# The causal mask of the diagonal blocks: added by VectorE in PSUM, not by a product on TensorE

## The reference, cut to what matters

```python
# x: (4, 2048, 256) float32
Q = sign(x * sign(bv_q)); K = sign(x * sign(bv_k)); V = x * sign(bv_v)
scores = einsum('btd,bsd->bts', Q, K) * 256 ** -0.5
scores = where(causal, scores, -inf)
attn = where(causal, sigmoid(scores * 4.0), 0.0)
x = layernorm(x + einsum('bts,bsd->btd', attn, V))
# then: top-1 routing over 32 experts with a capacity, silu(g) * u, down, residual, layernorm
```

## Time and profile before

| | |
|---|---|
| median of the runs | 556.41 us (556.22 to 556.51, 3 runs) |
| span of the profiled execution | 556.1 us |
| TensorE busy | 523.5 us (94%) |
| VectorE busy | 407.6 us (73%) |
| ScalarE busy | 378.5 us (68%) |
| GpSimd busy | 373.8 us (67%) |
| the mask's products, L897 | 64, mean 219 ns |

### The profile page before, as it was taken

One profiled execution on the slowest core, in us unless ns is written; L12 is line 12 of the kernel. 1 busy time (PEld: TensorE's weight loads), 2 busy tenths in 40 slices (PEclk: granted clock), 3 DMA queues, 4 the chain that ended last, 5 costly groups with the idle time before them and its releaser, 6 DMA issues.

```text
span 556.1 us, 12156 instructions
## 1 busy us (share of the span) xinstructions
PE 523.5 (94%) x3990; PEld 458.8 (82%) x4028; DVE 407.6 (73%) x1026; ACT 378.5 (68%) x775; POOL 373.8 (67%) x497
## 2 busy tenths in 40 slices
PE   6999999999999999999999889999999999999970
PEld 5889888898988888988988448888888888888860
DVE  3774878866678857779575637888788888888870
ACT  5886968869778778688686306667667767677640
POOL 4647868777867778786773541677776777676772
PEclk9999999999999999999999999999999999999995
DMA  8994332254332632247911043666777776683200
GB/s 256 374 327 174 82 96 59 82 166 98 115 74 78 165 96 86 62 104 205 317 52 60 18 134 63 187 200 191 214 207 212 204 218 208 210 251 90 61 33 35
DMA packets 91902, 81.52 MB, mean 147 GB/s; under 512 B 31626, under 2 KB 83066, under 8 KB 91840
## 3 DMA queue, kind: packets, MB, share of 16 engines
q1 hardware_dynamic: 84848, 66.39, 41.3%
q0 software_dynamic: 6912, 14.30, 7.6%
q10 hardware_dynamic: 80, 0.07, 0.0%
HBM read 44.33 MB, written 37.90 MB: 148 GB/s over the span
## 4 chain that ended last, share of the span: by engine, by line
PE 84%; DVE 5%; issue 4%; POOL 3%; DMA 1%; ACT 1%; another core or an unknown queue 1%; DVEq 0%; POOLq 0%; SPq 0%; ACTq 0%
PE ps L918 11%; PE ps L919 10%; PE ps L920 10%; PE ps L894 9%; PE ps L1074 8%; PE ps L1082 7%; PE ps L1075 7%; PE ps L1100 5%; PE ps L1108 3%; PE ps L1047 2%; PE ps L937 2%; PE ps L1097 2%; PE ps L1099 1%; PE ps L1098 1%; DVE hl_ring L1170 1%
## 5 line engine op out<-in xcount | busy, mean ns | idle before, releaser
L918 PE MATMUL ps<-v_hl,hl_ring 128*128 128x256 f32 x544 | 175.8, 323 | 0.3 <-DVE hl_ring L1170 0.3
L919 PE MATMUL ps<-v_hl,hl_ring 128*128 128x256 f32 x544 | 153.4, 282 | 0.0
L920 PE MATMUL ps<-v_hl,hl_ring 128*128 128x256 f32 x544 | 153.1, 281 | 0.0
L918 PEld LDWEIGHTS ps<-v_hl,hl_ring 128*128 128x128 f32 x544 | 103.3, 190 | 15.8 <-issue 2.1
L1170 DVE TENSOR_TENSOR hl_ring<-ps,hl_ring 128x512 fp32r<-128x512 f32 (+3 forms) x160 | 93.3, 601 | 20.0 <-ACT ps L695 16.0
L919 PEld LDWEIGHTS ps<-v_hl,hl_ring 128*128 128x128 f32 x544 | 103.6, 190 | 2.4
L920 PEld LDWEIGHTS ps<-v_hl,hl_ring 128*128 128x128 f32 x544 | 103.2, 190 | 0.0
L693 ACT ACTIVATE hl_ring<-ps 128x512 fp32r<-128x512 f32 (+3 forms) x160 | 85.9, 537 | 20.5 <-PE ps L894 9.4
L695 ACT ACTIVATE ps<-ps 128x512 f32<-128x512 f32 (+3 forms) x160 | 87.1, 544 | 0.0
L619 POOL DMA_INDIRECT out_dram<-alone,ids x55 | 69.3, 1260 | 24.5 <-issue 18.8
L535 POOL DMA_INDIRECT expert_rows<-xrow,slot x64 | 64.3, 1005 | 29.2 <-issue 24.9
(11 more groups left out here) (163 smaller groups left out, 1095.8 us busy)
## 6 DMA issues: line engine op xcount, KB each, us to landing
expert_rows<-xs SPq DMA_DIRECT2D x40, 258.0 KB, 5.2
xs<-expert_rows SPq DMA_DIRECT2D x32, 258.0 KB, 3.1
xall<-in_L_attn_x_dram SPq DMA_DIRECT2D x16, 512.0 KB, 4.9
out_dram<-alone SPq DMA_DIRECT2D x16, 512.0 KB
xall<-in_L_ffn_w_gate_dram SPq DMA_DIRECT2D x32, 256.0 KB, 4.5
xall<-in_L_ffn_w_up_dram SPq DMA_DIRECT2D x32, 256.0 KB, 4.7
xall<-in_L_ffn_w_down_dram SPq DMA_DIRECT2D x32, 256.0 KB, 5.1
xs<-expert_rows SPq DMA_DIRECT2D x31, 64.5 KB
```

The source lines that it names most:

```text
L918: mm(o, ah, v_hl[:, 0, j, :], start=(j == 0 and i % 2 == 0), stop=False, skip_group_check=True)
L919: mm(o, ah, v_hl[:, 1, j, :], start=False, stop=False, skip_group_check=True)
L920: last = mm(o, al, v_hl[:, 0, j, :], start=False, stop=(j == GT * g + i), skip_group_check=True)
```

## The change

TensorE's third product of a diagonal step is gone. VectorE gets a new function, `mask(n)`: on a diagonal step it waits for the scores of step n and adds the mask to the 128 columns of the diagonal block, in place in PSUM; it signals `masked`. ScalarE's sigmoids of a diagonal step wait for `masked` and no longer for `scores_ready`. VectorE issues `mask` three steps ahead: right behind `low` of step n it stands for step n + 3, over the end of a batch too, ahead of whatever the tables put at step n; those of the first three steps stand in the prologue.

```diff
+AHEAD_MASK = 3
...
+        def masks_to(n):
+            return NT // B * (n // NS) + sum(j >= GT * g for g, j in STEPS[:n % NS])
...
 def weights(b, k):
-                act.wait_ge(scores_ready, n + 1)
+                if j >= GT * g:
+                    act.wait_ge(masked, masks_to(n) + 1)
+                else:
+                    act.wait_ge(scores_ready, n + 1)
...
 def scores(b, k):
-                diag = j >= GT * g
                 for c in range(DC):
                     last = mm(o, k_t[:, c, j * P:(j + 1) * P], q_t[:, g, c, lo:GQ],
-                              start=(c == 0), stop=(c == DC - 1 and not diag))
-                if diag:
-                    last = mm(ps[:, k % SB, lo:lo + P], identb[:, :], maskb[:, :], start=False, stop=True)
+                              start=(c == 0), stop=(c == DC - 1))
                 last.then_inc(scores_ready, 1)
...
+            def mask(n):
+                g, j, lo = cols(n % NS)
+                if j >= GT * g:
+                    dve.wait_ge(scores_ready, n + 1)
+                    o = ps[:, n % NS % SB, lo:lo + P]
+                    v_.tensor_tensor(o, o, maskb[:, :], ALU.add).then_inc(masked, 1)
...
 def batch(b, first, last):
                 for k in range(NS):
                     low(b, k)
+                    if b * NS + k + AHEAD_MASK < B * NS:
+                        mask(b * NS + k + AHEAD_MASK)
...
             v_.tensor_scalar(k_t[:, 1, 0:GQ], q_t[:, 0, 1, :], qk_sgn[:, 1:2], None, ALU.mult).then_inc(key_first, 1)
+            for n in range(AHEAD_MASK):
+                mask(n)
             dve.wait_ge(vh_first, 1)
```

More of the change, by code:

```diff
@@ L195, in bass_postln_attn_moe_kernel @@
         scores_ready = sem("scores_ready")
+        masked = sem("masked")
         a_ready = sem("a_ready")
```

## The result

| | before | changed |
|---|---|---|
| median of the runs | 556.46 us (556.22 to 556.55, 4 runs) | 564.86 us (563.75 to 569.01, 4 runs) |
| ratio, 95% interval | | 1.0164 (1.0132 to 1.0195) |
| span of the profiled execution | 556.1 us | 563.2 us |

The changed kernel is 8.4 us slower. The prediction was 568.7, with 560.3 to 576.5 as its range. The direction was right and the range holds the result, but the forecast loss was 12.3 us. The two places that should have made it up did not share it as predicted: one cost more, the other nothing. A later set of runs gave 575.8 for the same kernel, and there the second place cost what was predicted. Most of what follows is about that.

A forecast was written before the change was run, and what follows sets the result against it. TensorE was taken to bound the kernel. Terms -1.1 - 0.4 + 0.5 + 7.5 + 5.1 + 0.7 = +12.3 us on the 556.1 span gave 568.4, with 0.3 for the median 568.7 us; range 560.3 to 576.5.

The forecast's parts named there:

- The two places: Three batch ends, +7.5 us, and steps 17 to 20 of three batches, +5.1 us: predicted losses from VectorE waiting for scores.
- What bounds the kernel: Attention, four batches: TensorE bounds it, so removing 64 mask products there can win at most 6.2 us.
- (a): Three batch ends: next batch's first mask delays the gate, GpSimd, ScalarE and VectorE's subtraction; 2.5 us each, +7.5.
- The clock falls: Rival, chance 0.12: after the batch-end wait TensorE's clock halves, 2.5 us more at each of three boundaries; 576.2 us.
- (b): Steps 17 to 20: step 20's mask meets a late TensorE signal ahead of the router's pick; +1.7 in three batches, +5.1.
- signals in time: Rival, chance 0.22: the delay at steps 17 to 20 does not meet the new wait; 562.7 us.
- The first batch: Steps 17 to 20 of batch 1: no late signal there, so it keeps its saving of 0.39 us.
- (c): Steps 33 to 36: step 37's mask and the pick make S(39), step 39's scores, 0.25 late; +0.7 for four batches.
- (d): Steps 5 to 8: nothing comes late, 0.28 us kept in each of four batches, -1.1.
- (e): Kernel start: first sigmoid waits for a mask, three masks precede VectorE's first-values work; between 0.2 and 0.8, taken +0.5.

The follow-up runs named there:

- the most that can be won: The kernel before with its 64 mask products left out and nothing in their place, so diagonal blocks are unmasked: 553.88 us, ratio 0.9944.
- the filler kernel: The changed kernel plus 11 unused products of 512 columns on TensorE ahead of S(4), the scores of step 4, at three batch ends: 571.35 us.
- the last set: The changed kernel, nothing altered, run again on another chip beside the kernel before at 556.50 us: 564.64 and 564.94 us, ratio 1.0149.

## Why the prediction was right or wrong

*What bounds the kernel.* Right: where masks cost nothing, the time goes below before. The 6.2 us of "the most that can be won" was a count of groups, not of the path; 3.3 were measured. The sum did leave the saving out at the three batch ends, and it has none for the first group of batch 1 either, without a reason; without masks that group gives 0.01.

*(a) The batch end.* The chain over four engines and its durations held to 0.1 us in T(0), and moving two masks took 7.9 us back. Three boundaries at 2.7 and not 2.5 is 0.6 off. The step that was mis-sized is the 0.24 us of spare time that I took off in front of S(4). V(0) behind it waits for the residual sums (0.83 us from their start to its first product before, 0.82 after), and these have no spare time: they came the whole 2.5 later with T(0), and 0.21 more for the mask between. The term was 7.5 and measured 10.7; the other 2.6 are the clock.

*The clock falls.* I gave it 0.12 as a case of its own at 7.5 us. It fell at two of three boundaries for 3.4 us and cost 1.3 each time, as the filler kernel shows. The mechanism was right, the size was three times too large, and it is no case beside the others: it comes on top of (a). The Trainium skill, "TensorE: Matmul & The Clock Gate", section "HAM oscillation — how this bites in real kernels", describes a kernel that waits some 3 to 5 us between groups of products, and whose clock falls at every such wait. Here shorter waits, 2.65 us, did it at two of three places.

*(b) Steps 17 to 20.* In the first and the last set this step failed: -0.3 in place of +5.1, and the rival "signals in time", at 562.7, was the true case. I had read a delay of the trace of before as fixed to the step. It is real, the runs point to the scatter's traffic as its source, and the size was right (1.72, 1.77 and 1.79 for 1.73) where it occurs; but whether it occurs is not the kernel's alone. The argument "it stands at the same step in three batches" showed that it was systematic in one execution, no more.

*The first batch.* Predicted to keep 0.39, it lost 1.1. I asked what stands behind the mask at step 17 and not at step 20. There stands the copy of the fourth query group, which TensorE needs for S(24):

```profile
49.08 0.68 DVE L1157 COPY q_t<-ps 128x1024 bf16<-128x1024 bf16 x1
...
49.82 0.11 PEld L902 LDWEIGHTS ps<-q_t,k_t 128*128 128x128 bf16 x2 [1.52 <-DVE q_t L1157]
```

This is after, first set; in before the copy started at 46.33. With all masks behind the other work the stretch is -0.39; with only that of step 20 moved, +0.5.

*(c) Steps 33 to 36.* Predicted a loss of 0.2 a batch, it kept 0.4 where signals were in time; where they were late it cost 0.2 to 0.3 in batches 2 and 3. The estimate rested on the earlier trace rows, which contains a late signal, and so was right for that case alone, and not for batch 1, where the port and the clock made it 3.5. *(d)* was right to 0.1. *(e)* was at the lower bound, 0.2.

*The range.* Its lower end takes 2.4 off "signals in time", but the terms named for that (0.3 at the start, 0.7 for (c), little for the shorter masks) make about 1.1, and 2.7 if (c) keeps its saving as well. The result lies above either end.

*The sum.* Off by: (a) and clock +3.2, (b) -5.4, first batch +1.5, (c) -2.5, (e) -0.3, and -0.5 at S(29) of batch 2. There TensorE waited 0.64 us for a subtraction in before (0.45 with the scatter's traffic left out) and not at all in the changed kernel; why is open. That is -4.0, from +12.3 to +8.2 but for rounding. That the median came within 4 us of the forecast is partly luck: errors of 3 to 5 us cancelled.

## What to carry to other kernels

When an instruction that waits is put into an in-order queue, list everything behind it at every place, once per table entry, and give the new instruction the last place that its reader allows; here that alone turned 3.2% slower into 0.26% faster. Before counting a saving, leave the work out and look: 6.2 us on paper were 3.3, since four groups of sixteen gave nothing: three sit under another engine's chain, and one at the start. A slack that hides a delay in the kernel before isn't room: look in more than one execution for signals that come late, and keep them away from a queue with work behind.

## What the runs showed of the hardware

- TensorE's signals can reach other engines some 2 us late (mostly 2.1 to 2.7 us after the step was taken up, in place of 0.65 to 0.70), one of them recorded together with the next step's. This happened while the transfers of GpSimd's scatter were due. With one-row transfers in their place no signal of step 20 was late in three traces; the clear case is the kernel before, where all nine cases with the scatter were. It came and went between sets of the same kernel, and what decides was not found.
- Equal waits of 2.65 us without a product were followed by 3.4 us at the 1.2 GHz level in two of three cases, 1.3 us each, and at the same two places when the changed kernel ran again in the third set. In the set at 575.8 it was all three, once for 6.8 us.
- A VectorE multiplication from SBUF to SBUF went from 0.34 to 3.11 us beside GpSimd work that left a gap of 0.02 us at most, and ended 0.16 us after it.
